# Eight SBUF-to-SBUF block transposes per tile on SyncE's queue, and the input rows loaded a second time for layer 2

## The reference

```python
def transformer_conv(x, src, dst, Wq, bq, Wk, bk, Wv, bv, Ws, bs, H, C, concat):
    q = (x @ Wq + bq).reshape(n, H, C)      # k and v alike
    alpha = jnp.einsum('ehc,ehc->eh', q[dst], k[src]) / jnp.sqrt(C)
    p = jnp.exp(alpha - segment_max(alpha, dst)[dst])
    denom = segment_sum(p, dst) + 1e-16
    out = segment_sum(p[:, :, None] * v[src], dst) / denom
    out = out.reshape(n, H * C) if concat else out.mean(axis=1)
    return out + x @ Ws + bs
...
h = relu(transformer_conv(x, ..., H=4, concat=True))
out = transformer_conv(h, ..., H=2, concat=False)
return layernorm(x + out)
```

## Time and profile before

| | |
|---|---|
| time, median of 3 runs | 2586.89 us (2585.23 to 2589.06) |
| span of the profiled execution, first to last instruction | 2580.9 us |
| time of that execution outside its span | 6.0 us, by the median of the runs (2586.9 - 2580.9); it has no time of its own in the results |
| TensorE busy | 2360.8 us, 91% of the span |
| VectorE busy | 2026.2 us, 79% |
| ScalarE busy | 1651.1 us, 64% |
| GpSimd busy | 433.0 us, 17% |
| DMA queue 1 (SP), share of the 16 DMA engines | 19.1% |
| mean granted TensorE clock | 0.978 of 2.4 GHz |

### The profile page before, as it was taken

The page is one execution under the profiler, slowest core; times in us unless marked ns, Lnnn a source line. Parts: engine busy times, 40 slices in busy tenths (PEclk is TensorE's granted clock), DMA queues, the critical chain, the costliest instruction groups (busy, mean ns, idle before and its releaser), DMA issues. The chain is left out here.

```text
span 2580.9 us, 64168 instructions
## 1 busy us (share of the span) xinstructions
PE 2360.8 (91%) x18557; PEld 2004.2 (78%) x18558; DVE 2026.2 (79%) x6021; ACT 1651.1 (64%) x3383; POOL 433.0 (17%) x876
## 2 busy tenths in 40 slices
PE   2778888887999999999999999998789999999995
PEld 1356666666888888888888888888468999999995
DVE  5699999997888878888878878887237777777775
ACT  1689999995666666666666666665116665566653
POOL 4410000000211111121212111121011121211211
PEclk8889999999999999999999999999899999999998
DMA  2012222223211211112112112110312221222210
GB/s 71 1 59 87 87 86 86 86 86 93 54 31 33 55 34 36 48 34 54 30 34 54 30 34 54 33 31 9 134 42 68 63 73 48 73 60 61 73 48 26
DMA packets 46697, 141.98 MB, mean 55 GB/s; under 512 B 7621, under 2 KB 22828, under 8 KB 40249
## 3 DMA queue, kind: packets, MB, share of 16 engines
q1 hardware_dynamic: 43103, 136.94, 19.1%
q10 hardware_dynamic: 3396, 2.42, 0.4%
HBM read 91.34 MB, written 48.00 MB: 54 GB/s over the span
## 5 line engine op out<-in xcount | busy, mean ns | idle before, releaser
L1084 ACT ACTIVATE probT_l<-transposed_l 125x500 f16<-125x500 f32 (+1 forms) x1050 | 569.7, 543 | 669.5 <-PE transposed_l L1264 655.2
L1133 DVE CUSTOM_DVE_ANT_0 prob_l<-score_l,mask_l 125x500 f32<-125x500 f32 (+1 forms) x1050 | 649.8, 620 | 256.1 <-PE score_l L1239 210.6
L1239 PE MATMUL score_l<-KT,QT_l 128*125 128x500 f16 (+1 forms) x3150 | 771.1, 354 | 24.1 <-issue 17.6
L1145 DVE SCALAR_TENSOR_TENSOR probT_l<-transposed_l,probT_l 125x500 f16<-125x500 f32 (+1 forms) x1050 | 651.0, 620 | 125.4 <-ACT probT_l L1084 119.3
L1275 PE MATMUL output_l<-V,probT_l 125*125 125x256 f16 x3750 | 739.8, 275 | 0.0
L1277 PE MATMUL output_l<-V,probT_l 125*125 125x128 f16 x3750 | 680.9, 219 | 0.0
L1264 PEld LDWEIGHTS transposed_l<-ident,prob_l 125*125 125x125 f32 x3750 | 549.5, 188 | 91.8 <-DVE probT_l L1145 6.7
L1264 PE MATMUL transposed_l<-ident,prob_l 125*125 125x125 f32 x3750 | 589.5, 275 | 5.0 <-DVE probT_l L1145 5.0
L1077 ACT ACTIVATE prob_l<-prob_l,neg_max_l 125x1000 f32<-125x1000 f32 (+1 forms) x450 | 521.5, 1159 | 0.0
L1275 PEld LDWEIGHTS output_l<-V,probT_l 125*125 125x125 f16 x3750 | 512.3, 137 | 9.7 <-issue 0.2
L1277 PEld LDWEIGHTS output_l<-V,probT_l 125*125 125x125 f16 x3750 | 516.9, 138 | 0.0
(11 more groups left out here) (176 smaller groups left out, 1723.2 us busy)
## 6 DMA issues: line engine op xcount, KB each, us to landing
mask_l<-mask_scratch SPq DMA_DIRECT2D x48, 1367.2 KB
mask_scratch<-work SPq DMA_DIRECT2D x128, 273.4 KB
mask_l<-mask_scratch SPq DMA_DIRECT2D x48, 158.7 KB
hT_scratch<-rowsT_l SPq DMA_DIRECT2D x25, 250.0 KB, 2.2
hT<-hT_scratch SPq DMA_DIRECT2D x6, 1000.0 KB, 13.5
mask_scratch<-work SPq DMA_DIRECT2D x128, 31.7 KB
mask_l<-mask_scratch SPq DMA_DIRECT2D x2, 929.7 KB
xres<-in_x SPq DMA_DIRECT2D x1, 1562.5 KB
```

The source lines that it names most:

```text
L1084: act.activation(probT[:, p, 0, 0:b - a], flip_bank(h, p)[0:TP, 0:b - a], ACT.Copy, scale=P_UP).then_inc(s_hi, 1)
L1133: dve.tensor_tensor_reduce(out=prob[:, h % 2, a:b], in0=score_bank(h, p)[0:TP, 0:b - a], in1=mask[:, parity, a:b], scale=1.0, scalar=-3.0e ...
L1145: dve.scalar_tensor_tensor(probT[:, p, 1, 0:b - a], flip_bank(h, p)[0:TP, 0:b - a], P_UP, probT[:, p, 0, 0:b - a], ALU.mult, ALU.subtract) ...
L1239: last = pe.matmul(score_bank(h, p)[0:TP, 0:b - a], QT[:, h % 2, i, :], KT[:, h, j, a:b], start=n == 0, stop=n == len(parts) - 1)
```

## The change

There are two parts. In layer 1's attention SP issues eight DMA transposes per tile after the store of `rowsT`, 200 in all. Each reads `flip_from` (128 partitions of 1024 f16 elements, 256 KB, filled once with 1.0 by GpSimd) and writes one half of `flip_to` as eight transposed blocks of 128x128. Nothing reads `flip_to`. A transpose waits until the last but one before it has landed, so at most two are under way. SP waits for the fill of `flip_from` before the first mask load, and for all transposes at the end of the block.

To make room in SBUF, `xres` no longer lives through layer 1. In `mask_and_projections` x is in a tensor of that block (`x_rows`), and neither the load of bs2 nor the addition of it stands there any more. `projections2` loads x and bs2 again behind the loads of `hT`, and GpSimd adds them after its 25 casts.

```diff
@@ build
-        xres = sb("xres", [TP, NT, C])
...
+            xres = sb2("xres", [TP, NT, C])
@@ mask_and_projections
-        bs2_sb = sb("bs2_sb", [TP, C])
+        xres = sb("x_rows", [TP, NT, C])
...
-                act.dma_start(bs2_sb[:, :], bs2.partition_broadcast(TP)).then_inc(s_bias, 16)
...
-                pool.wait_ge(s_bias, 48)
-                pool.wait_ge(s_xtp, len(x_groups))
-                pool.tensor_tensor(xres[:, :, :], xres[:, :, :],
-                                   bs2_sb[:, :].unsqueeze(1).broadcast_to([TP, NT, C]), ALU.add).then_inc(s_const, 1)
...
-                dve.wait_ge(s_bias, 48)
+                dve.wait_ge(s_bias, 32)
@@ projections2
+                sp.dma_start(xres[:, :, :], x.rearrange("(t p) c -> p t c", p=TP)).then_inc(s_x, 16)
+                sp.dma_start(bs_sb[:, :], bs2.partition_broadcast(TP)).then_inc(s_x, 16)
...
+                pool.wait_ge(s_x, 32)
+                pool.tensor_tensor(xres[:, :, :], xres[:, :, :],
+                                   bs_sb[:, :].unsqueeze(1).broadcast_to([TP, NT, C]), ALU.add).then_inc(s_added, 1)
+                pool.wait_ge(s_added, 1)
@@ attention
+        wide = 8
+        flip_from = sb("flip_from", [C, wide * C], F16) if layer == 1 else None
+        flip_to = sb("flip_to", [C, 2, wide, C], F16) if layer == 1 else None
...
                     if layer == 1:
                         store_rowsT(t)
+                        for j in range(8):
+                            if j >= 2:
+                                sp.wait_ge(s_flip[j % 2], 64 * t + 16 * (j // 2)).then_inc(s_flip_seen, 1)
+                            elif not is_first(t):
+                                sp.wait_ge(s_flip[j % 2], 64 * t).then_inc(s_flip_seen, 1)
+                            sp.dma_start_transpose(flip_to[:, j % 2, :, :], flip_from[:, :]).then_inc(s_flip[j % 2], 16)
+                if layer == 1:
+                    sp.wait_ge(s_flip_from, 1)
...
                 if layer == 1:
                     sp.wait_ge(s_stored, 16 * NT)
+                    for i in range(2):
+                        sp.wait_ge(s_flip[i], 64 * NT)
...
+                if layer == 1:
+                    pool.memset(flip_from[:, :], 1.0).then_inc(s_flip_from, 1)
```

More of the change, by code:

```diff
@@ L118, in build @@
             }
-            mask_and_projections(nc, x, src, dst, Wk1, bk1, Wv1, bv1, Wq1, bq1, Ws1, bs1, bs2,
-                                 ident, xres, layer1, mask_dram)
+            mask_and_projections(nc, x, src, dst, Wk1, bk1, Wv1, bv1, Wq1, bq1, Ws1, bs1,
+                                 ident, layer1, mask_dram)
             attention(nc, 1, H1, 1, layer1, mask_dram, ident, hT_dram=hT_dram, h_max=h_max)
@@ L135, in build @@
             y = sb2("y", [TP, NT, C])
+            xres = sb2("xres", [TP, NT, C])
             stats = sb2("stats", [TP, NT, 6])
-            projections2(nc, Wk2, bk2, Wv2, bv2, Wq2, bq2, Ws2, layer2, hT_dram, h_max, ident)
+            projections2(nc, x, bs2, xres, Wk2, bk2, Wv2, bv2, Wq2, bq2, Ws2, layer2, hT_dram, h_max, ident)
             attention(nc, 2, H2, H1, layer2, mask_dram, ident, xres=xres, y=y, stats=stats)
@@ L234, in wait_scaled, with mask_and_projections @@
         eng.wait_ge(self.s_scaled, 6)
-def mask_and_projections(nc, x, src, dst, Wk, bk, Wv, bv, Wq, bq, Ws, bs, bs2,
-                         ident, xres, L, mask_dram):
+def mask_and_projections(nc, x, src, dst, Wk, bk, Wv, bv, Wq, bq, Ws, bs,
+                         ident, L, mask_dram):
     xT, KT, V = L["featT"], L["KT"], L["V"]
@@ L777, in _, with projections2 @@
                             add_zeros(u, 1, False).then_inc(s_cnt, 1)
-def projections2(nc, Wk, bk, Wv, bv, Wq, bq, Ws, L, hT_dram, h_max, ident):
+def projections2(nc, x, bs2, xres, Wk, bk, Wv, bv, Wq, bq, Ws, L, hT_dram, h_max, ident):
     hT, KT, V = L["featT"], L["KT"], L["V"]
@@ L801, in projections2 @@
         s_rows, s_dve = sem("bias2_rows_loaded"), sem("dve_chain2")
+        bs_sb = sb("bs2_sb", [TP, C])
+        s_x, s_added = sem("x2_loaded"), sem("x2_biased")
         scales = Scales(nc, sb, sem, 2, H2, H1, (Wk_sb, L["Wq"], Wv_sb), bv_sb,
@@ L936, in attention @@
         summed = sb("summed", [TP, 2, C])
+        wide = 8
+        flip_from = sb("flip_from", [C, wide * C], F16) if layer == 1 else None
+        flip_to = sb("flip_to", [C, 2, wide, C], F16) if layer == 1 else None
+        if layer == 1:
+            s_flip_seen = sem("flip_seen")
+            s_flip_from, s_flip = sem("flip_source_ready"), [sem("flipped_even"), sem("flipped_odd")]
         S = [bank(f"score{i}") for i in range(3)]
```

## The result

The changed kernel takes 2598.36 us (median of 4 runs, 2597.96 to 2600.13), the kernel before beside it 2586.7. The ratio is 1.0044, 95% interval 1.0028 to 1.006: 11.7 us slower, where 20.2 were forecast. The profiled execution took 2598.01 us with a span of 2596.1, so that 1.9 us lie outside a span. The profiled execution of before, with 2580.9, was thus, by an estimate, one of some 2582.8 us, 4 us under its median. Trace against trace the difference is 15.2 us, and only part of it is the change.

A forecast was written before the change was run, and what follows sets the result against it. TensorE was taken to bound layer 1's attention, with barriers deciding at the seams. Terms +18.2 + 0.9 + 7.2 - 6.1 = +20.2 us gave a span of 2601.1 and a time of 2607.1 us, range 2594 to 2640.

The forecast's parts named there:

- What bounds the kernel: Layer 1's attention: TensorE bound, busy 98%; SP waits 45.6 us a tile, room for transposes; seams between blocks cost time.
- Transposes at the end of the block: End of layer 1's attention: eight transposes after the last store delay the next block by 18.2 us (7.0 to 35.2).
- D: SP's time for eight transposes, to the last one's landing: taken as 20 us, between bounds of 8.8 and 37.
- The loop undisturbed: Layer 1's attention loop: transposes cost nothing while they take under 45.6 us a tile; rival with 1 us a tile, chance 0.09.
- 39 us late: Layer 1's loop: a mask load may come some 39 us late before VectorE feels it; 2 us late was forecast.
- The addition in `projections2`: End of the second projections: GpSimd's 7.45 us addition after the last cast delays the barrier, +7.2 us.
- The addition that is gone: First block: without GpSimd's addition VectorE is no longer held, mask windows begin 6.1 us earlier, a gain of 6.1 us.
- The fill: Start of layer 1's attention: first mask load waits for the memset of `flip_from`, paid once, +0.9 us.
- The span and the median: Profiled execution of before: span 2580.9 us, time by the runs' median 6.0 us more, added to the forecast span.
- SP as the bound: Rival, layer 1's loop: eight transposes over 45.6 us make SP set the pace, time about 3243 us or more; chance 0.13.
- Transposes as fast as other DMAs: Skill's statement, set against the slow rival: the lower bound of 8.8 us holds, sum +9.0 us, or 2595.9.
- the reading that eight blocks follow one another at the 1309 ns: Slow rival's case: eight blocks in each of eight transposes take 84 us a tile, giving 3593 us.

The follow-up runs named there:

- the run: The kernel before without GpSimd's addition of bs2 to xres in the first block, nothing else changed: 2582.86 us (12 runs), ratio 0.9981.

## Why the prediction was right, and where its sizes were off

- **What bounds the kernel**: right. The loop hid eight transposes a tile; TensorE's time and the turn of the loop are the same, and the cost came at the seams. SP's wait before the mask loads shrank as forecast, to 2.6 us a tile.
- **Transposes at the end of the block**: mechanism right, size off. Forecast D = 20 and +18.2, measured D = 14.4 and +12.8. This is the mis-sized term, and it makes 5.4 of the 8.5 us between forecast and result. Of the bounds (8.8 from a store's landing and 37 from pieces of 32 bytes) the lower was the nearer: the packets are of 256 bytes, and cost 22 ns each, not 8.5. The middle had nothing else for it; that the time fell within the range is owed to the width of the range.
- **The loop undisturbed**: right for the changed kernel (2.5 us by medians, not to be told from 0), but my reason, that a mask load doesn't slow TensorE's matmuls, looked at the wrong place. What gets longer is the stop at the turn back, and the changed kernel escapes that as its transposes end 23 us ahead of it. Nor can the mask load be 39 us late: with sixteen transposes it is 12 us late, VectorE never waits for a mask, and the loop loses 32 us.
- **The addition in `projections2`**: +7.2 forecast, +6.7 at the seam, some 5 net, for the start of layer 2's attention gives 1 to 2 us back. The addition does meet VectorE's last subtraction, which the prediction named as a danger; the hold ends with the addition.
- **The addition that is gone**: -6.1 forecast, -4.5 in the trace and -4.9 in the run. The step that failed is that VectorE's next row would follow at once; 1.2 us of its own delay had been hidden behind the held subtraction. What that delay waits for stays open. The forecast start of the matmul, 134.4, came out at 134.05 by luck: 1.9 us of its 6.4 were there ahead of the addition's place.
- **The fill**: +0.9 forecast, 0.95 us in the row, the first masked piece 1.2 us later.
- **The span and the median**: I put 6.0 us between them. It is 1.9 in the changed kernel; the rest would be that the profiled execution of before was some 4 us under its median.

With the measured terms the sum is 12.8 + 0.95 + 5 - 4.9 = 13.9 us, inside what the ratio allows (7.2 to 15.5). The two additions were both put too high, the loss by some 2 us and the gain by 1.2; that these nearly cancel in the sum is luck. SP as the bound did not come about: it needs 24 a tile or more. Transposes as fast as other DMAs, which the Trainium skill (Advanced Engine Details and Errata, "X-Bar Transpose (TRN2)") states, don't agree with the rows: 158 GB/s here, and 177 with four under way, against 376 in the earlier trace rows. Nor does the reading that eight blocks follow one another at the 1309 ns that the Trainium skill (VectorE: DVE Perf Modes, "The three transpose paths") gives for one: eight blocks take 14.4 / 8 = 1.8 us in a row of transposes.

Part of the spread between executions is visible too. Before has one turn of 50.1 us among ten, the others 48.0 to 48.6, the changed kernel none, the one without the last tile's transposes five. In such a turn the clock is down to half, 1.2 GHz, for 3.4 us behind the stop, which costs 1.9 us. The window of before:

```profile
1525.00:1528.40 3.40, 3.40 (x17) 2.94 (x17) 1.19 (x3) 0.59 (x1) 0.76 (x3) 0.50 0.03 7
```

By an estimate, five such turns are 9.5 us, about as much as the executions of one kernel differ by; no two traces of the same kernel are there to show it.

## What to carry to other kernels

A queue with room in a loop hides an added transfer there, but the same transfer after the last iteration stands before the barrier in full: cost the last iteration by itself, and put it ahead of the last store, where its step at the end was gone (2.56 us; for the last iteration alone this wasn't tried). Room must be counted for the DMA engines as well as for the issuing queue, and a transfer may be in time for its reader and still do harm by where it comes to lie, here just ahead of the packet of instructions that TensorE's stop waits for. A long GpSimd operation goes in pieces into its gaps, not in front of a barrier.

## What the runs showed of the hardware

- A transpose of a 128x1024 block of 16-bit values is 1024 packets of 256 bytes. SP is busy for 1.26 us with its issue and it lands after 3.2 us. Eight at the end of the block take 14.4 us with two under way, 1.8 each; with four under way they take 12.8, 1.6 each (from 1802.10 to 1814.9). Beside a load of 1.5 MB one takes 2.3 to 2.9 us.
- At the loop's turn back TensorE stands still for 1.5 to 2.2 us without a releaser. With transposes under way it was 1.6 to 2.6, with a mask load issued some 8 us ahead 2.0 to 4.8. Each stop ends 1.6 to 2.0 us after a packet of 16,384 bytes of an instruction queue (q8, 121 packets and 1.98 MB in both kernels) has arrived, in 140 of 140.
- Behind such a stop the granted clock sometimes falls to half of full speed, that is 1.2 GHz, for 3.4 us: after 1 stop of 10 in before, after 8 of 10 (once for 6.8 us) with sixteen transposes a tile, whose stops were 2.0 to 4.8 us long.
- While GpSimd's addition ran, VectorE's subtractions with both inputs in SBUF took 7.05 us for two (0.88 without it) and 7.13 us for one (0.42 without it). The Trainium skill (SBUF — State Buffer, "Who interferes with whom") has the rule, that such an instruction contends with a GpSimd one that reads SBUF; the traces agree, twice.
